# A graph-attention and mixture kernel on one Trainium2 core: the first normalisation and four projections placed ahead of the counting's control words

## The reference, cut to what matters

```python
x = x + gnn0(layernorm(x))    # q, k, v = h @ W; softmax over the edges of a node; weighted sum of v
x = x + ffn0(layernorm(x))    # 8 experts, the two best of each row
x = x + gnn1(layernorm(x))    # sum over edges, product with W, norm, gelu
x = x + ffn1(layernorm(x))    # 6 experts, the best of each row
```

## Time and profile before

| | us |
|---|---|
| median of 3 runs (lowest, highest) | 1057.72 (1057.11, 1058.36) |
| the profiled execution's own time | 1058.73 |
| its span in the trace | 1057.0 |
| start, until PE begins projection 2 | 33.67 |
| ten counting blocks | 153.66 |
| last counts, logs and first scores, until the attention's loop starts on PE | 40.87 |
| all that follows | 828.80 |

### The profile page before, as it was taken

One profiled execution on the slowest core, in us unless ns is written; L12 is line 12 of the kernel. 1 busy time (PEld: TensorE's weight loads), 2 busy tenths in 40 slices (PEclk: granted clock), 3 DMA queues, 4 the chain that ended last, 5 costly groups with the idle time before them and its releaser, 6 DMA issues.

```text
span 1057.0 us, 15755 instructions
## 1 busy us (share of the span) xinstructions
PE 876.7 (83%) x5230; PEld 592.0 (56%) x5231; DVE 587.3 (56%) x1798; ACT 372.6 (35%) x673; POOL 170.2 (16%) x269
## 2 busy tenths in 40 slices
PE   5999999879999999999890089999479999706990
PEld 2465554447777777777690067777234465604650
DVE  6578699149988777777513045555263067630112
ACT  1243343336665666666420033334100111202430
POOL 4000000000000000000004612222383034440004
PEclk9999999989999999999955599999879999657995
DMA  8914334563250000000096563332244213023326
GB/s 255 385 49 96 71 82 85 113 153 94 73 182 27 25 2 25 26 25 2 9 351 165 163 156 100 101 100 97 71 128 117 70 60 119 1 70 107 121 97 195
DMA packets 81503, 110.16 MB, mean 104 GB/s; under 512 B 39370, under 2 KB 48746, under 8 KB 81168
## 3 DMA queue, kind: packets, MB, share of 16 engines
q1 hardware_dynamic: 67984, 93.72, 30.0%
q0 software_dynamic: 13440, 15.43, 5.5%
HBM read 64.31 MB, written 44.76 MB: 103 GB/s over the span
## 4 chain that ended last, share of the span: by engine, by line
PE 77%; POOL 6%; DVE 5%; issue 4%; DMA 4%; ACT 2%; POOLq 0%; DVEq 0%; SPq 0%; ACTq 0%
PE ps L648 11%; PE ps L561 9%; PE ps L572 9%; PE ps L586 9%; PE ps L712 8%; PE ps L443 6%; PE ps L638 5%; PE ps L405 5%; PE ps L448 3%; PE ps L513 2%; PE ps L655 2%; POOL slots_d L1061 2%; PE ps L737 2%; DMA slots_d<-XN,slot 1%; PE ps L524 1%
## 5 line engine op out<-in xcount | busy, mean ns | idle before, releaser
L648 PE MATMUL ps<-R_B,R_A 128*128 x432 | 127.5, 438 | 1.3 <-ACT R_A L927 0.8
L888 ACT ACTIVATE R_A<-R_A,neg_max 125x1250 f32<-125x1250 f32 x80 | 106.6, 1333 | 58.2 <-DVE neg_max L1328 58.2
L561 PE MATMUL ps<-R_B 64*125 64x417 f32 (+1 forms) x480 | 107.3, 547 | 9.2 <-DVE neg_max L1328 6.6
L1328 DVE CUSTOM_DVE_ANT_0 R_A<-ps,R_B,neg_max 125x417 f32<-125x417 f32 (+1 forms) x160 | 97.7, 649 | 13.0 <-PE ps L561 13.0
L572 PE MATMUL ps<-ident,R_A 125*125 125x125 f32 x800 | 98.9, 278 | 0.0
L586 PEld LDWEIGHTS ps<-R_W,XN 125*64 125x64 f32 x1600 | 85.3, 136 | 24.1 <-issue 24.1
L572 PEld LDWEIGHTS ps<-ident,R_A 125*125 125x125 f32 x800 | 94.9, 188 | 1.8 <-DVE R_W L1335 0.7
L586 PE MATMUL ps<-R_W,XN 125*64 125x125 f32 x1600 | 94.7, 272 | 0.9 <-DVE X L1356 0.6
L648 PEld LDWEIGHTS ps<-R_B,R_A 128*128 128x128 f32 x432 | 78.8, 193 | 22.3 <-issue 14.9
L1237 DVE TENSOR_SCALAR R_B<-R_B 125x625 bf16<-125x625 uint16 x200 | 88.5, 443 | 0.0
L1038 POOL TENSOR_SCALAR rstd<-mv 125x10 f32<-125x10 f32 x1 | 0.2, 213 | 503.6 <-DVE mv L1182 503.6
(11 more groups left out here) (214 smaller groups left out, 1319.8 us busy)
## 6 DMA issues: line engine op xcount, KB each, us to landing
R_B<-in_L_ffn_w_dram SPq DMA_DIRECT2D x28, 512.0 KB, 6.9
R_A<-slots_d SPq DMA_DIRECT2D x42, 256.0 KB, 2.8
made_d<-R_A SPq DMA_DIRECT2D x42, 256.0 KB, 2.0
slots_d<-R_B SPq DMA_DIRECT2D x1, 6912.0 KB, 21.4
counts_d<-R_A SPq DMA_DIRECT2D x10, 546.9 KB
logs_d<-R_B SPq DMA_DIRECT2D x10, 546.9 KB
R_B<-logs_d SPq DMA_DIRECT2D x10, 546.9 KB
R_B<-counts_d SPq DMA_DIRECT2D x10, 546.9 KB
```

Source lines behind the costliest of these rows:

```text
L561: pe.matmul(bank(2 * h + g % 2, P, z - a), QT[r:r + DH, j, i * P:i * P + P], KT[r:r + DH, j, a:z], start=True, stop=True).then_inc(S("s_ma ...
L648: ins = pe.matmul(bank(b, TM, width), lhs[:, c * TM:c * TM + TM], flat[:, bass.ds(e * (n * width) + c * width, width)], start=c == 0, stop ...
L888: act.activation(SC[u % 2][h], SC[u % 2][h], ACT.Exp, bias=neg_max[:, 2 * (u % 2) + h:2 * (u % 2) + h + 1], scale=-1.0, accum_out=den[:, 2 ...
L1328: dve.tensor_tensor_reduce(SC[u % 2][h][:, a:z], bank(2 * h + g % 2, P, z - a), LNB[i % 2][:, a:z], -1.0, least if t else 3.0e38, ALU.add, ...
```

## The change

- DVE does the whole first normalisation before the control words instead of after them.
- PE forms the two small sums of the control words (L400) after the last turn of the normed rows instead of at the start, does projections 2 and 3 ahead of the branch, and waits there for the control word; ACT moves 2 and 3 ahead of its branch. The control sums use bank 4 instead of bank 7, which projection 2 now needs.
- `PROJECTED_AT` gives the blocks the projections 4 to 25, two each but for blocks 2 and 5, which have three (before: 2 to 26, three in blocks 0 to 4 and two in the others).
- After the ten blocks, projection 26 stands before the last `turn_counts` and 27 to 31 after it (before: 27 to 29, then 30 and 31). ACT converts the last counts ahead of any projection's move.
- Projection 32 stands before the third part of the first scores, 33 after it (before: both after it).

The diff, without the general branch (not taken here) and with the moved DVE functions, whose text is the same, left out:

```diff
-PROJECTED_AT = ((2, 5), (5, 8), (8, 11), (11, 14), (14, 17), (17, 19), (19, 21), (21, 23), (23, 25), (25, 27))
+PROJECTED_AT = ((4, 6), (6, 8), (8, 11), (11, 13), (13, 15), (15, 18), (18, 20), (20, 22), (22, 24), (24, 26))
...
-            pe.matmul(bank(7, T, 320), ones[0:80, 0:T], span_diag.rearrange("p k q -> p (k q)"),
+            pe.matmul(bank(4, T, 320), ones[0:80, 0:T], span_diag.rearrange("p k q -> p (k q)"),
                       start=True, stop=True).then_inc(S("span_sums"), 1)
-            pe.wait_ge(S("span_step"), 8)
-            for k in range(2):
-                ins = pe.matmul(bank(7, 1, T, 320 + 16 * k), spans[:, 6 + k:7 + k], ident[0:T, 0:T],
-                                start=True, stop=True)
-            ins.then_inc(S("ctl_sums"), 1)
+
...
             project(1)
             for i in range(5, T):
                 turn_normed(i)
+            pe.wait_ge(S("span_step"), 8)
+            for k in range(2):
+                ins = pe.matmul(bank(4, 1, T, 320 + 16 * k), spans[:, 6 + k:7 + k], ident[0:T, 0:T],
+                                start=True, stop=True)
+            ins.then_inc(S("ctl_sums"), 1)
+            project(2)
+            project(3)
+            pe.wait_ge(S("ctl_ready"), 1)
             all_hold = pe.value_load(ctl[0:1, T:T + 1], min_val=0, max_val=1)
...
-                for n in range(27, 30):
-                    project(n)
+                project(26)
                 turn_counts(T - 1)
-                for n in range(30, 32):
+                for n in range(27, 32):
                     project(n)
...
-            scores(0, (0, 1, 2))
-            for n in range(32, 34):
-                project(n)
+            scores(0, (0, 1))
+            project(32)
+            scores(0, (2,))
+            project(33)
             pe.wait_ge(S("qkv_moved"), 34)
...
             move_projected(1)
             for i in range(5, T):
                 move_normed(i)
+            move_projected(2)
+            move_projected(3)
+            act.wait_ge(S("ctl_ready"), 1)
             all_hold = act.value_load(ctl[0:1, T:T + 1], min_val=0, max_val=1)
...
-                move_projected(27)
                 copy_counts(T - 1)
-                move_projected(28)
-                move_projected(29)
+                move_projected(26)
                 counts_and_logs(T - 1, (T - 1) % 2)
-                for n in range(30, 32):
+                for n in range(27, 32):
                     move_projected(n)
...
             dve.wait_ge(S("idx_turned"), 1)
             link(dve.tensor_copy(idxT.rearrange("p k (q r) -> p k r q", r=2),
                                  bank(6, EP, 480).rearrange("p (k r q) -> p k r q", k=3, r=2)))
+            for i in range(T + 3):
+                if i < T:
+                    first_stats(i)
+                if 1 <= i <= T:
+                    first_moments(i - 1)
+                if i >= 3:
+                    first_rows(i - 3)
             dve.wait_ge(S("span_sums"), 1)
-            least, greatest = bank(7, T, ET), bank(7, T, ET, ET)
+            least, greatest = bank(4, T, ET), bank(4, T, ET, ET)
...
             dve.tensor_copy(ctl[:, 0:T + 1], ctl_f[:, 0:T + 1]).then_inc(S("ctl_ready"), 1)
-            for i in range(T + 3):
-                if i < T:
-                    first_stats(i)
-                if 1 <= i <= T:
-                    first_moments(i - 1)
-                if i >= 3:
-                    first_rows(i - 3)
             dve.wait_ge(S("ctl_ready"), 1)
```

More of the change, by code:

```diff
@@ L505, in _ @@
                     general_block(b)
-                for n in range(2, 32):
+                for n in range(4, 32):
                     project(n)
@@ L1156, in _ @@
                                  bank(6, EP, 480).rearrange("p (k r q) -> p k r q", k=3, r=2)))
-            dve.wait_ge(S("span_sums"), 1)
-            least, greatest = bank(7, T, ET), bank(7, T, ET, ET)
[L1160 to L1164, removed]
-                                          ALU.is_ge, ALU.mult), 2)
-            step(dve.scalar_tensor_tensor(span_tmp[:, 3, :], span_tmp[:, 2, :], -BIG, span_tmp[:, 1, :],
-                                          ALU.mult, ALU.add), 3)
-            dve.tensor_tensor(span_tmp[:, 4, :], span_tmp[:, 2, :], span_tmp[:, 0, :], ALU.mult)
-            step(dve.tensor_reduce(spans[:, 2:3], span_tmp[:, 3, :], X_AXIS, ALU.min), 4)
-            step(dve.tensor_reduce(spans[:, 3:4], span_tmp[:, 4, :], X_AXIS, ALU.max), 5)
-            step(dve.tensor_tensor(spans[:, 4:5], spans[:, 3:4], spans[:, 2:3], ALU.subtract), 6)
-            step(dve.tensor_scalar(spans[:, 6:7], spans[:, 2:3], float(ET - WIN), 0.0, ALU.min, ALU.max), 7)
-            step(dve.tensor_scalar(spans[:, 7:8], spans[:, 4:5], float(WIN - 1), None, ALU.is_le), 8)
-            dve.wait_ge(S("ctl_sums"), 1)
-            link(dve.tensor_copy(ctl_f[:, 0:T], bank(7, 1, T, 320)))
-            link(dve.tensor_reduce(ctl_f[:, T:T + 1], bank(7, 1, T, 336), X_AXIS, ALU.min))
-            dve.tensor_copy(ctl[:, 0:T + 1], ctl_f[:, 0:T + 1]).then_inc(S("ctl_ready"), 1)
             def row_stats(source, i):
@@ L1219, in _, with step @@
                     first_rows(i - 3)
+            dve.wait_ge(S("span_sums"), 1)
+            least, greatest = bank(4, T, ET), bank(4, T, ET, ET)
+            def step(ins, n):
+                ins.then_inc(S("span_step"), 1)
+                dve.wait_ge(S("span_step"), n)
+            step(dve.tensor_scalar(span_tmp[:, 2, :], least, spans[:, 1:2], None, ALU.is_lt), 1)
+            step(dve.scalar_tensor_tensor(span_tmp[:, 2, :], greatest, spans[:, 0:1], span_tmp[:, 2, :],
+                                          ALU.is_ge, ALU.mult), 2)
+            step(dve.scalar_tensor_tensor(span_tmp[:, 3, :], span_tmp[:, 2, :], -BIG, span_tmp[:, 1, :],
+                                          ALU.mult, ALU.add), 3)
+            dve.tensor_tensor(span_tmp[:, 4, :], span_tmp[:, 2, :], span_tmp[:, 0, :], ALU.mult)
+            step(dve.tensor_reduce(spans[:, 2:3], span_tmp[:, 3, :], X_AXIS, ALU.min), 4)
+            step(dve.tensor_reduce(spans[:, 3:4], span_tmp[:, 4, :], X_AXIS, ALU.max), 5)
+            step(dve.tensor_tensor(spans[:, 4:5], spans[:, 3:4], spans[:, 2:3], ALU.subtract), 6)
+            step(dve.tensor_scalar(spans[:, 6:7], spans[:, 2:3], float(ET - WIN), 0.0, ALU.min, ALU.max), 7)
+            step(dve.tensor_scalar(spans[:, 7:8], spans[:, 4:5], float(WIN - 1), None, ALU.is_le), 8)
+            dve.wait_ge(S("ctl_sums"), 1)
+            link(dve.tensor_copy(ctl_f[:, 0:T], bank(4, 1, T, 320)))
+            link(dve.tensor_reduce(ctl_f[:, T:T + 1], bank(4, 1, T, 336), X_AXIS, ALU.min))
+            dve.tensor_copy(ctl[:, 0:T + 1], ctl_f[:, 0:T + 1]).then_inc(S("ctl_ready"), 1)
             dve.wait_ge(S("ctl_ready"), 1)
```

## The result

The changed kernel takes a median of 1051.7 us (20 runs, 1046.2 to 1056.0) against 1057.8 us before (20 runs, 1055.9 to 1060.0): ratio 0.9943, 95% interval 0.9930 to 0.9955. In a later set of six runs, beside its variants, it gave 0.9919 (0.9904 to 0.9934). So by the two ratios the change gains 6 to 8.6 us. The forecast was a gain of 10.7 us and a time of 1047.0, with a range up to 1051.5; the measured median lies 0.2 us outside it. Two of all the timed runs were much slower at a lower mean clock (1068.1 us at 0.865 in `e4_again`, 1246.2 us at 0.718 among the runs of the kernel before), and all ratios and ranges leave them out.

The account below looks back on a forecast made before the run. PE's order was taken to set the time, busy 876.7 of 1057.0 us. Start -3.1, counting +7.4 and the part behind it +6.4 summed to 10.7 us gained: median 1047.0, range 1044.5 to 1051.5.

Parts of the forecast that it names:

- the end: From PE's last tile to the attention's loop: 34.5 us instead of 40.87, with PE never waiting for the logs; 6.4 less.
- The rival that the turns would not come sooner: Last counts: ACT or DVE holds the turn, the end gives back its 6.4, gain 4.3, median 1053.4; chance 0.04.
- the start of the sum: Up to projection 4: PE begins it at 36.8 instead of 33.67, with projections 2 and 3 already done.
- Projections 0 and 1 take 8.4 us: Start: sixteen matmuls, the first four near 0.86 us each, counted in the 36.8 for projection 4.
- projection 2's slow start: Behind the branch gap, projection 2 took 5.37 us, not 3.44; following the turns at once, it would save 1.93.
- The prediction's count of the blocks: Blocks 0 and 1, up to the opening of window 2: 29.3 us instead of 34.64.
- Projection 0 was forecast at 17.8: Start: W's first part lands at 17.8, later than five turned rows at 16.9, and sets projection 0's start.
- The rival of a start at 20.74: Head: W's first part or x lands late and projection 0 still starts at 20.74; gain 7.8, median 1049.9; chance 0.13.
- The stage behind, taken as unchanged: Behind the loop's start: not touched, shifts as a whole and keeps its 828.8 us.
- Half clock after the turns, or the branch uncovered: Start, around projection 2 and the branch: costs 1.1 to 3.4 us; with 1.9, gain 8.8, median 1048.9; chance 0.17.
- The rival of half clock in paced blocks: Counting blocks where PE waits for tiles: one block at half clock costs 12.1 us, two give 1071.2; chance 0.05.

Follow-up runs that it names:

- e4_again: A second run of e4_busy_head, the changed kernel with idle products on PE ahead of projections 0 and 1: ratio 0.9902 to the kernel before.
- e8_scores_old: Changed kernel with projections 32 and 33 again behind all three parts of the first scores: 1052.4 us, ratio 0.9932 to the kernel before.
- e1_head: Changed kernel's head and blocks, with projection 26 put in block 9 and the end as before: 1059.9 us against 1059.7, ratio 1.0002.
- e4_busy_head: Changed kernel with idle products on PE ahead of and between the first five turns: 1047.4 us, ratio 0.9885 to the kernel before.
- e6_busy_tail: Kernel before with the new end and the idle products on PE, without the moved normalisation and projections: 1048.1 us, ratio 0.9894.
- before_look_1: One more profiled execution of the unedited kernel before: 1055.6 us.
- look_1: One more profiled execution of the unedited changed kernel: 1052.9 us.
- e5_busy_all: e4_busy_head with idle products also between the tiles of blocks 2, 7 and 8, giving up those counts' values: 1054.1 us, ratio 0.9950.
- e7_branch_early: Changed kernel with the control word read before projections 2 and 3, which go back into the blocks: 1050.6 us, ratio 0.9920 to the kernel before.
- look_2: A further profiled execution of the unedited changed kernel: 1052.4 us.
- after_again: Unedited changed kernel run again beside its variants: 1051.1 us, ratio 0.9919 to the kernel before.
- e2_tail: Kernel before with only the new end and one projection less in the blocks: 1049.8 us against 1059.7, ratio 0.9901.
- e3_late_rows: Changed kernel with the ten reads of the count rows held until DVE has combined unit 0's scores: 1050.0 us, ratio 0.9914.

## Why the prediction was wrong

**The direction, and the end: right.** Projection 26 ahead of the turns, the turns at +4.4 to +4.5, five projections over the transfers, no wait for the logs, an end of 34.5 us: of the twelve profiled executions with early turns, ten have an end between 34.3 and 34.8. In the other two (the first profile with 37.6, and `e8_scores_old` with 38.4) PE stood for 1.14 us and its clock fell. The rival that the turns would not come sooner is refuted.

**The step that failed is the start of the sum.** The prediction let the start and the blocks up to window 2 gain 2.2 us (68.31 to 66.1) and the head 2.3 in all; `e1_head` measured 0. Two terms, both read from one execution, carry the difference.

The first is "Projections 0 and 1 take 8.4 us". They took 10.15 in the profile after and 9.4 to 10.2 in its four profiles. In `e4_busy_head` and `e6_busy_tail`, where PE is kept busy first, all sixteen matmuls took 7.11, so they are slow because PE has stood before them. Why they are slower in one execution than in another is not shown. The earlier start alone isn't it: the nine profiles with the moved normalisation and no idle products lie between 8.7 and 10.2 (9.6 on the mean), the four with the old one between 8.5 and 8.9.

The second is projection 2's slow start, 1.93 us that the new order was to save. Two further profiles of the kernel before don't have it. The first of them, on the timeline:

```profile
33.79 3.67 PE L443 MATMUL ps<-XT,R_W 128*128 128x512 f32 x8 [1.11 <-issue]
```

Projection 2 takes 3.67 us there, also behind a gap of 1.11 us, and the same 3.67 in the second. So window 2 opened at 66.7 and 67.0, and not at 68.3. Before's end was shorter in them too, 39.7 and 39.8, since the clock rose again sooner in it:

```profile
186.82 10.37 PE ps L448 x24
...
214.31 2.26 PE ps L561 x4
216.56 4.60 PE ps L448 x8
...
226.39 1.67 PE ps L561 x8
```

(4.60 us for the slow part of projections 32 and 33 instead of the 5.89 of the earlier trace rows.) Together they put before's loop 1.2 to 1.8 us earlier in these two profiles, though 0.75 us are lost again to a falling clock in block 8. This doesn't show that the first execution was an odd one: its 1058.7 us are 0.9 above the median of twenty runs, the two later ones' 1055.6 are 2.2 below it.

**The head moves the loop by nothing.** By the table, the changed kernel's window 2 opens at 67.3 to 68.0, against 66.7 to 68.3 before. In all 17 profiles it opens 6.1 us behind the first turned counts on PE, with the moves, the logarithm and the mask between, and from projection 2 up to that turn PE works without a wait. On the timelines, first of before_look_1, then of look_1:

```profile
60.64 1.31 PE L416 MATMUL ps<-ident,R_A 125*125 125x125 f32 x10
...
66.73 0.23 DVE L1242 TENSOR_SCALAR R_B<-R_B,tile_off 125x20 f32 x1
```

```profile
31.70 10.57 PE L439 MATMUL ps<-XT,R_W 128*128 128x512 f32 x24
...
61.95 1.31 PE L412 MATMUL ps<-ident,R_A 125*125 125x125 f32 x10
...
68.04 0.23 DVE L1247 TENSOR_SCALAR R_B<-R_B,tile_off 125x20 f32 x1
...
69.15 0.66 PE L401 MATMUL ps<-R_B 125*125 125x512 bf16 x1 [2.65 <-DVE R_B L1242]
```

Before, five full projections (2 to 6) stand between the turned rows and this turn, in the changed order six (2 to 7). So PE needs 30.25 us from projection 2 to the turn instead of 26.85 (60.64 - 33.79): the 3.4 us more eat what the earlier start and the missing gap bring, 2.7 and 1.1 us. Before, projection 7 filled PE's time while window 2 was on its way; now PE stands for 2.65 us there. The prediction's count of the blocks had this extra projection in it (29.3 forecast, 29.42 measured), so without the slow start there was next to nothing to gain. By window 2 both orders have done projections 0 to 7, and with 26 out of the blocks the rest takes 117.0 to 118.1 us, whichever table is used (without the idle products of `e5_busy_all`).

`e7_branch_early` bears this out from the other side: it has before's order of projections, window 2 opens 6.09 us behind its turn as well, and what PE lost ahead of it shows in full, less the projection that isn't there.

**A number that was right by another path.** Projection 0 was forecast at 17.8, because W's first part was to be the later one and five turned rows ready at 16.9. In the profile x came 1.0 us late for the statistics, and PE's matmul was released by the move of the fifth block, which ended at 17.87. In look_2 that move ended at 18.30 and projection 0 began at 18.45; in `e4_busy_head`, at 17.41 and 17.55. So it follows the rows, W was in by 17.55 in that profile, and 18.01 next to 17.8 is partly luck. The rival of a start at 20.74 did not occur.

**The stage behind, taken as unchanged.** It was 826.9 to 828.8 before and 828.2 to 831.4 after (830.1 on the mean). Up to 329 us behind the loop's start all profiles agree within 0.1 us. Then comes the routing, where PE stands for some 45 us, and the clock, at half when PE starts again, rises at different times. The windows of before_look_1 and of look_1 from PE's restart on (columns as above, the last but two is the clock):

```profile
602.00:604.00 2.00, 1.12 (x4) 0.72 (x4) 0.00 (x0) 0.39 (x1) 0.00 (x0) 0.50 0.66 240
...
606.00:608.00 2.00, 2.00 (x8) 1.57 (x8) 0.00 (x0) 0.04 (x1) 0.00 (x0) 0.60 0.00 0
```

```profile
596.00:598.00 2.00, 1.10 (x4) 0.72 (x4) 0.00 (x0) 0.00 (x0) 0.00 (x0) 0.50 0.91 333
...
606.00:608.00 2.00, 2.00 (x6) 1.55 (x6) 0.00 (x0) 0.00 (x0) 0.00 (x0) 0.50 1.03 288
608.00:610.00 2.00, 1.82 (x11) 1.27 (x9) 0.43 (x2) 1.12 (x3) 0.52 (x1) 0.99 1.03 265
```

In twelve profiles the clock rose 5 to 7 us behind the restart; in after_again, look_1, look_2, `e4_again` and `e5_busy_all` it rose 10 to 11 us behind it, and their next step of the experts is longer (4.1 to 4.5 us instead of 3.0 to 3.1). They are also the five with the longest stage, 830.3 to 831.4. It doesn't come from the earlier loop: `e2_tail`, `e3_late_rows`, `e4_busy_head`, `e6_busy_tail` and `e7_branch_early`, with loops at 216.1 to 220.1, don't have it. What decides it is open.

**Sum.** The time was forecast 4.7 us too low (1047.0 against 1051.7), and the median before was as the forecast took it (1057.8 against 1057.7), so the miss of the time is in the new kernel's stages (projection 2's slow start is not among them, since the new kernel doesn't have it; it only swelled the gain that was counted against the first execution of the kernel before). Their forecast ends at 1046.3 in the trace; the four profiles end at 1050.7 on the mean. Of these 4.4 us, 1.4 are projections 0 and 1, 0.3 their start (18.15 on the mean instead of 17.8), 0.5 the blocks and what else lies ahead of the end, block 4 with 15.42 instead of 15.07 among them, 0.8 the gap and the fall of the clock in one of four ends, and 1.3 the stage behind. The profile made with the first twenty runs divides otherwise: 1.75 for projections 0 and 1, 3.1 in the end, and nothing behind. With three executions before and four after, the shares are rough.

The range has a slip as well: "a gain of 6 to 13.2" reaches up to 1051.7, not 1051.5, and the measured gain is 6.1.

**Half clock after the turns, or the branch uncovered**, given 0.17, did not occur in the changed kernel: 24 matmuls in 10.57 us and no gap. Against its reading, PE is busy in the turns for 2.73 of 3.43 us before (29.11 to 32.54), not for half of the time.

**The rival of half clock in paced blocks**, given 0.05, did occur as an event: the clock fell in block 2 in all four profiles, in block 7 in two and in block 8 in one, and in the two further profiles of the kernel before in blocks 7 and 8. The fall in block 2 belongs to the change: all eleven profiles with six projections ahead of the first turn have it, behind PE's 2.65 us for window 2, and none of the six with five. What it costs depends on the block. One paced by DVE has room for it: 13.95 to 14.44 us instead of 13.95 to 14.06, and up to 14.72 in the variants. One whose second projection is full has less. Both kinds, in before_look_1 (windows):

```profile
143.97:158.18 14.21, 12.51 (x66) 8.97 (x66) 13.00 (x46) 5.37 (x10) 0.00 (x0) 0.88 0.45 89
158.18:174.00 15.82, 14.67 (x64) 8.48 (x65) 13.09 (x45) 5.19 (x8) 0.00 (x0) 0.89 0.35 79
```

Block 7 is as long as at full clock to 0.15 us (14.06), block 8 took 15.82 us instead of 15.07: 0.75 us, where the prediction had priced such a block at 12.1 more. The clock was at half for only some 3.5 us of it (0.11 x 15.82 / 0.5), not for the whole block.

The Trainium skill (TensorE: Matmul & The Clock Gate, A second HAM failure mode: psum-queue depth-cycling) says that short idles between groups of matmuls can make the clock swing; the falls in the paced blocks agree (clock 0.88, with 2.65 us of PE standing ahead of the one in block 2), and the blocks at 1.00 in the earlier trace rows had merely not shown them.

**What stays open:** the 1.14 us gap inside the first scores (in the first profile and in `e8_scores_old`, not in the ten others with early turns), and whether 0.9943 in one set of twenty runs and 0.9919 in a later one of six are different at all, as their intervals overlap. The runs of the first set go with the mean granted clock (1046.2 us at 0.912, 1056.0 at 0.901), so what differs from run to run is likely the clock, but where it falls in each is not recorded.

## What to carry to other kernels

Before summing from one profiled execution, mark each of its stretches at half clock, and ask whether it belongs to the order of the work or to that execution; a second profile of the same kernel was 3 us away from the first one here. When work is moved ahead of a stage, count what then stands ahead of the first step on which another engine waits. Here that was the first turned counts; it got a sixth projection ahead of it, and PE got a wait of 2.65 us behind it, where a projection used to be. What pays is a long round trip (turn, store, load) started first, with the independent work of the bottleneck engine put behind it and not ahead of it.

## What the runs showed of the hardware

Projections 0 and 1 ran at about 0.86 us a matmul for four to eight matmuls, against 0.43 for 24 in 10.37 us, while the granted clock read 1.00 in these rows; with PE kept busy before, all sixteen took 7.11 us. So in these rows the clock's column doesn't show the slow matmuls, and the durations do. Falls of the clock came in blocks in which PE waits in small steps for DVE's tiles (busy for 12.76 of 13.97 us and 12.48 of 14.07, clock 0.88), but not in each of them: the changed kernel's block 8, with 12.62 of 14.04, stayed at 1.00 in the first profile. The block as a whole must not be priced at half clock: before_look_1's block 8 lost 0.75 us. After PE had stood for some 45 us, the clock rose again 5 to 7 us behind its restart in twelve profiles and 10 to 11 us behind it in five. Reading the word and branching took DVE 3.4 us in the changed kernel and 2.3 before, with the same instructions.
